# Local attention with norms in column tiles and raw q and k read from PSUM, and a state-space scan that reads PSUM

## The reference

```python
def attn_layer(x, Wqkv, qs, ksc, Wo):
    qkv = x @ Wqkv
    q, k, v = jnp.split(qkv, 3, -1)                 # 16 heads of 64
    q = l2norm(q) * qs
    k = l2norm(k) * ksc
    q = q * cos * scale + rotate_half(q) * sin * scale
    k = k * cos * inv + rotate_half(k) * sin * inv
    out = local_attention(q, k, v)                  # windows of 32, each sees itself and the one before
    return out @ Wo

def ffn_layer(x, g, bln, W1, b1, W2, b2):
    xn = (x - mu) / jnp.sqrt(var + 1e-05) * g + bln
    a, gate = jnp.split(xn @ W1 + b1, 2, -1)
    return a * jax.nn.gelu(gate, approximate=False) @ W2 + b2
```

```python
def step(h, inp):
    d_t, x_t, B_t, C_t = inp
    A_bar = jnp.exp(d_t[:, :, None] * A)
    h = A_bar * h + (d_t * x_t)[:, :, None] * B_t[:, None, :]
    y_t = jnp.einsum('bdn,bn->bd', h, C_t)
    return (h, y_t)
```

## Time and profile before

| | us |
|---|---|
| median of 2 runs | 2734.66 (2733.21 to 2736.12) |
| the profiled execution, its own time | 2734.42 |
| its span, from the first to the last instruction | 2732.6 |
| busy: PE, DVE, ACT, POOL | 2391.9, 2401.9, 1988.0, 1164.5 |

### The profile page before, as it was taken

How to read it: one execution, slowest core, us unless ns; L and a number is a source line. 1 busy time by engine, 2 the same in 40 slices (tenths; PEclk the granted TensorE clock), 3 DMA queues, 4 the chain that set the end, 5 groups by cost and what they waited for, 6 DMA issues and landing times. The chain is left out here.

```text
span 2732.6 us, 60708 instructions
## 1 busy us (share of the span) xinstructions
PE 2391.9 (88%) x23660; PEld 1246.6 (46%) x23660; DVE 2401.9 (88%) x2594; ACT 1988.0 (73%) x3169; POOL 1164.5 (43%) x465
## 2 busy tenths in 40 slices
PE   7789999999999999999999999999998765565778
PEld 2345555555555555555555555555554222122355
DVE  5799999999999999999999999999995799999542
ACT  4778888888888888888888888888886643333433
POOL 0444444444444444444444444444441066566130
PEclk8899999999999999999999999999999877678889
DMA  0100000000000000000000000000000100000001
GB/s 20 52 2 2 2 24 10 10 2 2 24 10 10 2 13 13 9 10 2 13 13 14 5 2 13 13 17 2 2 2 1 36 0 0 0 0 0 17 16 46
DMA packets 15995, 29.49 MB, mean 11 GB/s; under 512 B 3616, under 2 KB 6064, under 8 KB 15664
## 3 DMA queue, kind: packets, MB, share of 16 engines
q1 hardware_dynamic: 15760, 25.78, 3.0%
HBM read 24.73 MB, written 1.05 MB: 9 GB/s over the span
## 5 line engine op out<-in xcount | busy, mean ns | idle before, releaser
L705 POOL TENSOR_TENSOR f_rot<-f_raw,f_tabc 128x1024 f32<-128x1024 f32 x192 | 453.0, 2360 | 925.3 <-DVE f_qk L753 583.6
L709 POOL TENSOR_TENSOR f_rot<-f_rot,f_shuf 128x1024 f32<-128x1024 f32 x192 | 452.4, 2356 | 235.6 <-DVE f_shuf L746 235.6
L746 DVE TENSOR_TENSOR f_shuf<-f_shuf,f_tabs 128x1024 f32<-128x1024 f32 x192 | 427.9, 2229 | 8.6
L776 DVE TENSOR_TENSOR f_s<-f_s,f_rcp 128x512 f32<-128x512 f32 x192 | 401.5, 2091 | 6.6
L604 ACT ACTIVATE f_raw<-f_ps 128x1024 f32<-128x1024 f32 x192 | 196.0, 1021 | 227.3 <-PE f_ps L425 227.3
L472 PEld LDWEIGHTS f_ps<-f_ptz,f_v 64*64 64x64 f32 x6144 | 259.1, 133 | 146.9 <-issue 146.9
L1133 POOL TENSOR_TENSOR s_prod<-s_state,s_cs 128x1024 f32<-128x1024 f32 x64 | 234.1, 3677 | 169.4 <-DVE s_state L1211 142.3
L968 PE MATMUL s_ps<-s_prod,s_ident 128*128 128x512 f32 x256 | 183.0, 872 | 132.7 <-POOL s_prod L1133 132.7
L595 ACT ACTIVATE f_v<-f_ps 64x256 f32<-64x256 f32 x768 | 287.0, 374 | 6.7
L472 PE MATMUL f_ps<-f_ptz,f_v 64*64 64x96 f32 (+1 forms) x6144 | 285.4, 243 | 2.3 <-ACT f_ptz L625 2.3
L424 PE MATMUL f_ps<-f_xs,f_wq 128*128 128x512 f32 x384 | 211.8, 633 | 71.1 <-ACT f_rn L613 47.1
(11 more groups left out here) (266 smaller groups left out, 3961.3 us busy)
## 6 DMA issues: line engine op xcount, KB each, us to landing
e_w<-in_e_w SPq DMA_DIRECT2D x16, 256.0 KB, 2.8
f_wq<-in_f_wq SPq DMA_DIRECT2D x12, 256.0 KB, 2.6
f_wk<-in_f_wk SPq DMA_DIRECT2D x12, 256.0 KB, 3.4
f_wv<-in_f_wv SPq DMA_DIRECT2D x12, 256.0 KB, 3.6
f_wo<-in_f_wo SPq DMA_DIRECT2D x6, 512.0 KB, 3.3
f_w<-in_f_w SPq DMA_DIRECT2D x6, 341.0 KB, 2.9
s_dx<-in_k_pick SPq DMA_DIRECT2D x1, 1536.0 KB, 9.1
f_w<-in_f_w SPq DMA_DIRECT2D x6, 192.0 KB, 3.2
```

Source lines behind the costliest of these rows:

```text
L705: pool.tensor_tensor(view(rot, 0, [S, 4], [1, S]), view(raw, 0, [S, 4], [1, S]), view(tab_c, 0, [S, 2], [0, 2], [1, S]), ALU.mult).then_in ...
L709: pool.tensor_tensor(rot[:, :], rot[:, :], shuf[:, :], ALU.add).then_inc(sem["rot"], 1)
L746: dve.tensor_tensor(view(shuf, 0, [S, 4], [1, S]), view(shuf, 0, [S, 4], [1, S]), view(tab_s, 0, [S, 2], [0, 2], [1, S]), ALU.mult).then_i ...
L776: dve.tensor_tensor(view(t, 0, [64, 8], [1, 64]), view(t, 0, [64, 8], [1, 64]), view(rc, 0, [1, 8], [0, 64]), ALU.mult).then_inc(sem["p"], 1)
```

## The change

In local attention:

- `raw` is gone. ACT squares straight from PSUM (`square`). DVE shuffles q and k from PSUM (`shuffle`) and multiplies q and k in PSUM with the cosine table (the new `straight`, after `soft_b`). POOL now multiplies the shuffled copy with the sine table and adds (`rotate`). `project` of the next pair waits for `sq`, `shuf` and `straight` of this one, where it waited for `ln`.
- `norms` uses 64 columns of the matrix of ones, one product for q into partitions 0 to 63 of bank 2 and one for k into partitions 64 to 127. Each head's norm stands on 32 partitions. `inverse_norm` is a Ln and an Exp of 512 columns into one of two `root` tiles. SP copies each 32 partitions of `root` twice into one of two `rn` tiles (`widen`: eight DMAs of 64 KB for each pair, 1536 in all, on the queue that also carries the weights). `normalise` waits for these DMAs. On PE `norms` come before `turn`, on ACT `inverse_norm` before `spread`.
- `values` is four products of 64 weight columns and 256 moving columns, into the two halves of the partitions, and ACT's four copies become one.
- The exponentials go to banks 4 and 5, and `soft_b` reads them there. So `scores` wait for `p` of the pair before (the end of `soft_b`) instead of `shift`.
- `variance` uses bank 3; the weights are loaded between the DMAs of `widen`.

In state space:

- Four blocks (h, k) run one after the other, 16 states each: 64 steps of one spread, drive, decay, scan, product and sum. B is spread anew for each k.
- DVE reads B straight from PSUM; the copy of B is gone. The decays are written to PSUM (one buffer) and the scan reads them there. State, product and the copy of C have two buffers.

```diff
-        raw, sq, shuf, rot, rn = (m.sb(f"f_{n}", 2 * UNIT) for n in ("raw", "sq", "shuf", "rot", "rn"))
+        sq, shuf, rot = (m.sb(f"f_{n}", 2 * UNIT) for n in ("sq", "shuf", "rot"))
+        rn = [m.sb(f"f_rn{b}", 2 * UNIT) for b in range(2)]
+        root = [m.sb(f"f_root{b}", UNIT) for b in range(2)]
...
+        def widen(sp, t, q):
+            gather(sp, sem["root"], t + q + 1)
+            gather(sp, sem["qk"], t + q - 1)
+            for c in range(2):
+                for h in range(2):
+                    for half in range(2):
+                        to, of = 64 * h + 32 * half, 64 * c + 32 * h
+                        sp.dma_start(rn[q % 2][to:to + 32, UNIT * c:UNIT * c + UNIT],
+                                     root[q % 2][of:of + 32, :]).then_inc(sem[f"wide{q % 2}"], 16)
...
-                pe.matmul(bank(2), xs[:, 128 * (q % 4):128 * (q % 4) + 128], wv[:, CH * (q // 4):CH * (q // 4) + CH],
-                          start=True, stop=True).then_inc(sem["v_mm"], 1)
+                for r in range(2):
+                    for h in range(2):
+                        at = 128 * (q % 4) + 64 * r
+                        mm = pe.matmul(view(ps, 2 * CH + 256 * r, [1, 256], p0=64 * h, rows=64), xs[:, at:at + 64],
+                                       view(wv, CH * (q // 4) + 64 * h, [128, 4], [1, 64]),
+                                       start=(r == 0), stop=True, skip_group_check=True)
...
-                pe.matmul(bank(0), same_head[:, :], sq[:, 0:UNIT], start=True, stop=True)
-                pe.matmul(bank(1), same_head[:, :], sq[:, UNIT:], start=True, stop=True).then_inc(sem["n_mm"], 1)
+                need(pe, sem["v"], i * 8 + j + 1)
+                for c in range(2):
+                    mm = pe.matmul(view(ps, 2 * CH, [1, CH], p0=64 * c, rows=64), same_head[:, 32:96],
+                                   sq[:, UNIT * c:UNIT * c + UNIT], start=True, stop=True, skip_group_check=True)
...
                 gather(sem["qk"], i * 8 + j + 1)
-                gather(sem["shift"], i * 8 + j)
+                gather(sem["p"], i * 8 + j)
...
-                    act.activation(s[j % 2][:, :], s[j % 2][:, :], ACT.Exp, scale=8.0).then_inc(sem["exp"], 1)
+                    act.activation(view(ps, 4 * CH, [CH, 2], [64, 4], [1, 64]), view(s[j % 2], 0, [64, 2], [128, 4], [1, 64]),
+                                   ACT.Exp, scale=8.0).then_inc(sem["exp"], 1)
...
                 if has:
-                    rotate(u, a)
+                    shuffle(u, a)
                 if before and j == 6:
                     hidden(k, 1)
                 if run:
                     soft_b(i, j)
+                if has:
+                    straight(u, a)
```

```diff
+            def step(h, k, i, n, par):
+                need(act, sem["scan"], i)
+                act.activation(view(ps, DB * CH + 1, [S, B // 2], [1, S - 1]),
+                               view(delta, k * T + h * H + 1, [S, B // 2], [1, S - 1]),
+                               ACT.Exp, scale=aneg[:, bass.ds(n, 1)]).then_inc(sem["decay"], 1)
+                act.wait_ge(sem["c_mm"], i + 1)
+                need(act, sem["prod"], i - 1)
+                act.activation(view(cs[par], 0, [1, H]), view(ps, CB * CH, [1, H]), ACT.Copy).then_inc(sem["c_in"], 1)
...
+            def drive(h, k, i, par):
+                dve.wait_ge(sem["b_mm"], i + 1)
+                need(dve, sem["prod"], i - 1)
+                dve.tensor_tensor(st[par][:, :], dx[:, k * T + h * H:k * T + h * H + H], view(ps, BB * CH, [1, H]),
+                                  ALU.mult).then_inc(sem["drive"], 1)
+
+            def scan(i, par):
+                dve.wait_ge(sem["drive"], i + 1)
+                dve.wait_ge(sem["decay"], i + 1)
+                dve.tensor_tensor_scan(st[par][:, :], view(ps, DB * CH, [1, H]), st[par][:, :], 0.0, ALU.mult,
+                                       ALU.add).then_inc(sem["scan"], 1)
```

More of the change, by code:

```diff
@@ new lines, in layer @@
+        def layer(sp, r, first, last):
+            for q in range(8 * NU):
+                widen(sp, r * 8 * NU, q)
+                if not first and q == 4:
+                    load_wo(sp, r, r * NU)
+                if not first and q == 9:
+                    load_w1(sp, r, r * NU)
+                if not first and q == 10:
+                    load_w2(sp, r, r * NU)
+                if not last and q == 8 * NU - 5:
+                    load_qkv(sp, r + 1, (r + 1) * NU, 0)
+                if not last and q == 8 * NU - 1:
+                    load_qkv(sp, r + 1, (r + 1) * NU, 1)
@@ L392, in _ @@
             load(sp, sem["const"], consts)
-            weights(sp, 0, 0)
-            with sp.Fori(1, DEPTH) as r:
-                weights(sp, r, r * NU)
+            for k in range(2):
+                load_qkv(sp, 0, 0, k)
+            load_wo(sp, 0, 0)
+            load_w1(sp, 0, 0)
+            load_w2(sp, 0, 0)
+            layer(sp, 0, True, False)
+            with sp.Fori(1, DEPTH - 1) as r:
+                layer(sp, r, False, False)
+            layer(sp, DEPTH - 1, False, True)
         @block.tensor
@@ L713, in slot @@
                 if has:
[L714 removed]
+                    rotate(u, a)
             iterations(pool, slot, lambda j: None)
@@ L902, in state_space @@
         added = m.sem("s_added")
-        D0, D1 = 2 * K, 2
+        BLOCKS = [(h, k) for h in range(2) for k in range(K)]
+        YB, DB, BB, CB = 0, 2, 4, 6
         body = ExitStack()
@@ L1068, in _ @@
             nc.scalar.preload_act_table_set(ACT_SET)
[L1070 to L1092 removed]
+            def step(h, k, i, n, par):
[6 more added lines that the diff above has]
+                act.activation(view(cs[par], 0, [1, H]), view(ps, CB * CH, [1, H]), ACT.Copy).then_inc(sem["c_in"], 1)
+            for b, (h, k) in enumerate(BLOCKS):
+                base = b * DS
+                act.wait_ge(sem["fin"], K * h + k + 1)
+                step(h, k, base, 0, 0)
+                step(h, k, base + 1, 1, 1)
+                with act.Fori(1, DS // 2) as n2:
+                    for par in range(2):
+                        step(h, k, n2 * 2 + (base + par), n2 * 2 + par, par)
+                if b == 0:
+                    soft(1)
             for c in range(NCH):
```

309 lines of the change are left out of this document (146 added, 163 removed).

## The result

The changed kernel takes 2921.4 us (2913.0 to 2929.7, 2 runs) for 2734.7 before: a ratio of 1.068, interval 1.055 to 1.082. It is 187 us slower, where 169 less were forecast.

What follows compares the result with a forecast made beforehand. It took PE and DVE as nearly full in the layers and DVE alone as the scan's limit; the DMA chain would set the new slot. 2734.4 - 110 (scan) - 58 (local attention) = 2566 us, range 2460 to 2685.

Steps and rivals of the forecast that it cites:

- T(s+2) = T(s) + E + 11.0: Local attention: scores of slot s+2 start at least E plus 11.0 us after those of s; iteration 80.5 us.
- E: Local attention: scores of slot s to end of norms of pair s+2, 6.7 + 0.86 n us, n other products before.
- Scan stage: State space: 64 steps of 3.6 us plus some 15 us, 245 us for 357, saving 110.
- the rival of a clock at 1.2 GHz: Scan stage: PE's clock stays at 1.2 GHz, a step takes 5.2 us, total 2668; chance 0.08.
- Halves overlap: Local attention, PE: products into different column halves run together, norms 0.86 us for 1.72; rival of no overlap, chance 0.04.
- The landing: Local attention: a DMA of inverse norms lands 1.8 us after its issue, ends 0.4 and 3.6.
- Two issues of SP stand 0.48 apart: Local attention: SP issues the eight DMAs of a pair 0.48 us apart, the last starting 3.3 us later.
- the rival with slow DMAs: Local attention: DMAs slower than forecast, 2662 us at 1 us more; chance 0.20 up to 2 us, 0.06 beyond.
- Values "stay at 0.86": Local attention, PE: the products of v in column tiles still take 0.86 us a slot.
- The wait for p: Local attention: scores wait for p, which DVE reaches only behind `normalise` and `shuffle`; 4.3 us from `normalise` to PE.
- The lower bound of a scan step, 3.33: Scan stage: 3.33 us a step with no semaphore seen, saving 128 us.
- DVE's 6.9 us a slot: Local attention: DVE's work falls from 9.1 to some 6.9 us a slot without the feed-forward pieces, no longer bounding.

Runs made afterwards that it cites:

- four_issues: Changed kernel with four DMAs of 64 partitions for each pair instead of eight of 32, norms reaching other heads than their own: 2701.1 us, ratio 0.987 to before.
- warm: Changed kernel with two added products of constants on PE ahead of the scores, behind the last Ln, in seven of eight slots: 2834.4 us, ratio 1.037 to before.
- no_dma: Changed kernel with the norms as two full products of 128 rows, two Ln and one Exp, no DMAs: 2764.6 us, ratio 1.010 to before.
- scan_only: Kernel before with only the new state-space part: 2629.3 us, ratio 0.961 to before.
- values_exp: Kernel before with the new state-space part, values in column tiles and exponentials in PSUM: 2911.4 us, ratio 1.064 to before.
- late_normalise: Changed kernel with `normalise` moved behind `soft_b` on DVE, ahead of `straight`: 2886.4 us, ratio 1.056 to before.

## Why the prediction was wrong

The path was right and its sizes were not. In the changed kernel `normalise` waits for a DMA and the scores wait for p, as forecast, but an iteration takes 95.0 us for 80.5. Two terms of T(s+2) = T(s) + E + 11.0 are mis-sized: the issues inside the 11.0, and E. Over the iterations between 300 and 1900, E sums to 42.7 us in the four even slots for the 33.7 of the chain, and the rest of the four links to 52.9 for 46.8 (four times 11.0, and the 2.8 added for slots 6 and 7 and for meetings). That is 9.0 and 6.1 us, and together the whole of what an iteration takes more (95.6 by these means).

- **Scan stage, right.** Forecast 245 us, measured 251.9; saved 105 for 110. Scans start 3.63 apart for 3.6, no DVE operation of the loop is held up by POOL. The clock is 0.96 in the loop, and the rival of a clock at 1.2 GHz fell.
- **Halves overlap, right.** The four passes of the norms start 1052.77 and the next work follows at 1053.78: 1.0 us, the 0.86 and a change of mode. The Trainium skill, TensorEngine Tiling (Array Packing), Key Properties, says that different tiles can execute in parallel; the trace agrees. The change of mode costs some 0.15 us here and decides nothing.
- **The landing, right.** 2.0 us at the median for 64 KB from SBUF to SBUF, where 1.8 was taken. The formula of the Trainium skill, DMA: Bandwidth & Descriptors, Anatomy of one DMA, which is for the software path, gives an estimate of 2.15 for 64 KB; the trace lies between the two.
- **"Two issues of SP stand 0.48 apart", wrong.** This is the first step that failed. The median is 0.63 and the mean 0.72, and in the link shown 0.66: there the stretch from Exp to `normalise` is 6.9 us for 0.2 + 3.3 + 1.8 = 5.3. The rest of that link held: 4.1 us of DVE for 4.3. With its 12.5 for 11.0 in four links, the step's own sum becomes 86.5 us an iteration for 80.5, so +86 us against before where -58 was forecast: the milder half of the rival with slow DMAs, in issue and not in landing. `four_issues` confirms the term, 220 us less with half of the issues.
- **"So T(s+2) is at least T(s) + E + 11.0", incomplete.** The measured iteration is 95.0; the remaining 8.5 us are in E. E was counted in PE's passes at full clock. But the chain lets PE idle 2 us ahead of the scores, and behind such gaps project takes 2.9 to 3.3 us for 1.9 and the values 0.3 to 0.7 more, three times an iteration, 5 us as an estimate. Idle time was treated as free. E of the slots 0, 2, 4 and 6 is 13.4, 9.2, 8.6 and 11.6 us for 9.3, 8.4, 6.7 and 9.3. In `warm`, at full clock, it is 10.8, 8.4, 7.0 and 9.8: 6.7 of the 9.0 us are gone, some 1.1 of them by the shorter hole. The rest of the links is 3.0 longer there.
- **Values "stay at 0.86", right in passes and wrong in code.** The hole in slot 0 costs 2.0 us an iteration and in the iteration shown stands ahead of one of the three drops of the clock. Nothing in the prediction looked at the number of instructions.
- **The wait for p.** The prediction had it only as the tail of the DMA chain. By itself it closes a ring through the next projection that costs 249 us in the order of before. In the changed order DVE has no table product ahead of p, and without the DMAs no mask product waits for p any more. So `no_dma` does not show this ring, and what it costs in the changed kernel apart from the DMAs is open. The 5.7 us an iteration between `no_dma` and `scan_only` lie for the most part in slot 0, 4.6 us with its hole and the half clock behind it. The order with `soft_b` behind `normalise` was not tried on the changed kernel, with or without DMAs.
- Two small sums are off and decide nothing. The lower bound of a scan step, 3.33, is 2.27 + 1.14 = 3.41 by its rows, which would save 123 and not 128 us. DVE's 6.9 us a slot would be 9.1 - 2.3 - 1.5 + 1.2 = 6.5.
- The range ended at 2685. It held neither slower issues together with lower clock, nor any price for p.

## What to carry to other kernels

Before a wait is moved from one operation to a later one (here from `shift` to p), write down the in-order queue of every engine on the way and close the ring back to the waiting instruction: if it passes through work that the waiting engine issues behind the wait itself, the two serialise, and moving one call may be the whole cure (2879 to 2632 us). Idle time of TensorE is not free: behind a gap of 2.0 us, `project` took 3.1 us for 1.9 and the values 1.5 for 1.0, so a change that takes work from a full PE but adds a wait can lose twice. Small DMAs issued in a row from one queue are priced by the issue, 0.6 to 0.7 us each, which no landing time shows.

## What the runs showed of the hardware

- Eight DMAs of 64 KB between SBUF partitions: 0.59 us median per issue and 5.6 for the eight in a row, 1.9/2.0/4.0 us to landing (min/median/max) on SP's queue; 0.48 had been read from two issues of weights. Given by ACT, they hold up ACT's own work, 112.6 us in 400 for four a pair.
- TensorE's granted clock in one profile: 1.00 over the layers while PE is busy 95% of the time; in the changed kernel 0.50 for 3.4 or 6.8 us behind 54 of its 72 gaps of 1.4 us or more. The Trainium skill, TensorE: Matmul & The Clock Gate, the part on the HAM clock gate, says that the clock is 1.2 GHz when the array has been idle and 2.4 GHz when it has been busy; the trace agrees, and shows the fall behind gaps as short as these.
- A hole of 1.5 to 2.8 us in the first scores of an iteration without a releaser (16 in 1600 us of the changed kernel, 31.5 us in all, one an iteration), in the kernels with the values in column tiles except `values_exp`, shorter (0.5 to 1.6 us) in `late_normalise` and the three with idle work, and in none without the tiles.
- An operation of DVE with one source in PSUM keeps its time beside POOL (p's product 0.69 us for 2.18, the drive 1.2 for 3.3); `normalise`, with two in SBUF, took 2.06 us at the median instead of 1.22 once `late_normalise` moved it beside POOL's products.
